# Mixes in four row strips, the first level ahead of the outputs, and a later logit stage

## The reference, cut to what matters

```python
xx = concatenate([zeros_like(x[:, :1]), x[:, :-1]], axis=1) - x
xxx = x + xx * maa_x
lora = tanh(xxx @ maa_w1).reshape(B, T, 5, 32)
m = einsum('btfd,fdc->fbtc', lora, maa_w2)      # mw, mk, mv, mr, mg
xw = x + xx * (maa_w + mw)                      # and xk, xv, xr, xg alike
r, k, v = xr @ Wr, xk @ Wk, xv @ Wv
g = tanh(xg @ gate_w1) @ gate_w2
w = time_decay + tanh(xw @ decay_w1) @ decay_w2
wdec = exp(-exp(w))
y = wkv6(r, k, v, wdec, u)                      # S = w*S + k v', y = r (S + u k v')
out = (norm(y) * g) @ Wo
```

## Time and profile before

| | us |
|---|---|
| median of three runs (lowest, highest) | 3041.12 (3040.53, 3043.16) |
| the profiled execution, whole time | 3043.45 |
| its span in the trace | 3041.6 |
| route a, up to the last scatter | 0 to 229 |
| experts a | 236 to 1164 |
| mix_and_route | 1171 to 2096 |
| experts b | 2101 to 3041 |

### The profile page before, as it was taken

How to read it: one execution, slowest core, us unless ns; L and a number is a source line. 1 busy time by engine, 2 the same in 40 slices (tenths; PEclk the granted TensorE clock), 3 DMA queues, 4 the chain that set the end, 5 groups by cost and what they waited for, 6 DMA issues and landing times. The chain is left out here.

```text
span 3041.6 us, 63629 instructions
## 1 busy us (share of the span) xinstructions
PE 2764.8 (91%) x21994; PEld 2212.3 (73%) x21994; DVE 1997.8 (66%) x4620; ACT 1575.5 (52%) x2733; POOL 1265.8 (42%) x1072
## 2 busy tenths in 40 slices
PE   6536999999999995899999999984999999999997
PEld 6535888888888883466666666663888888888886
DVE  5545666666666652688989898864666666566664
ACT  5424666666665652344444444432666656656663
POOL 2671322322222223457777777753222222232233
PEclk9999999999999997999999999997999999999998
DMA  9925545545544526201111111014455445445444
GB/s 343 334 94 116 91 81 89 94 77 88 95 78 86 96 33 222 98 16 44 35 53 33 54 33 55 26 38 116 82 89 95 77 86 95 79 86 94 80 70 149
DMA packets 540965, 281.28 MB, mean 92 GB/s; under 512 B 397591, under 2 KB 503131, under 8 KB 540480
## 3 DMA queue, kind: packets, MB, share of 16 engines
q1 hardware_dynamic: 478624, 202.67, 26.8%
q0 software_dynamic: 57888, 75.16, 14.6%
q10 hardware_dynamic: 4224, 0.52, 0.1%
HBM read 150.83 MB, written 146.41 MB: 98 GB/s over the span
## 5 line engine op out<-in xcount | busy, mean ns | idle before, releaser
L763 POOL DMA_INDIRECT acc_a<-ae_ob,ae_to x160 | 260.8, 1630 | 675.0 <-ACT ae_ob L712 623.0
L763 POOL DMA_INDIRECT acc_b<-be_ob,be_to x150 | 242.7, 1618 | 637.3 <-ACT be_ob L712 578.7
L730 ACT ACTIVATE be_h<-be_pH,b 128x512 f32<-128x512 f32 (+1 forms) x384 | 236.8, 617 | 359.2 <-PE be_pH L657 337.5
L730 ACT ACTIVATE ae_h<-ae_pH,b 128x512 f32<-128x512 f32 (+1 forms) x384 | 236.7, 616 | 342.1 <-PE ae_pH L657 324.1
L1478 POOL TENSOR_TENSOR m_xf<-m_tmp,m_xT 128x512 f32<-128x512 f32 x160 | 174.9, 1119 | 151.6 <-DVE m_tmp L1185 85.1
L1529 POOL DMA_INDIRECT slots_b<-m_row,m_sidx x128 | 143.1, 1118 | 109.3 <-issue 106.2
L1788 PEld LDWEIGHTS m_PP<-m_RP,m_KS 64*64 64x64 f32 x6656 | 115.6, 134 | 87.5 <-issue 86.4
L464 POOL DMA_INDIRECT slots_a<-ar_row,ar_sidx x128 | 126.0, 984 | 99.7 <-issue 73.8
L1788 PE MATMUL m_PP<-m_RP,m_KS 64*64 64x64 f32 x6656 | 130.0, 221 | 26.5 <-DVE m_A L1215 26.3
L657 PE MATMUL ae_pH<-ae_xT0h,ae_w_0h 128*128 128x512 f32 (+1 forms) x256 | 87.8, 343 | 69.3 <-DVE ae_xT0l L839 65.5
L1185 DVE SCALAR_TENSOR_TENSOR m_tmp<-m_B,m_ch,m_xx 128x512 f32<-128x512 f32 x160 | 114.0, 741 | 48.8 <-PE m_B L1895 38.5
(11 more groups left out here) (347 smaller groups left out, 9007.8 us busy)
## 6 DMA issues: line engine op xcount, KB each, us to landing
ae_stage<-in_w SPq DMA_DIRECT2D x64, 512.0 KB, 3.6
be_stage<-in_w SPq DMA_DIRECT2D x64, 512.0 KB, 3.5
slots_a<-empty SPq DMA_DIRECT2D x5, 4160.0 KB, 25.0
slots_b<-empty SPq DMA_DIRECT2D x5, 4160.0 KB, 31.6
ae_xq<-slots_a SPq DMA_DIRECT2D x252, 64.0 KB, 2.7
be_xq<-slots_b SPq DMA_DIRECT2D x252, 64.0 KB, 2.7
ar_xin<-in_x SPq DMA_DIRECT2D x16, 512.0 KB, 10.0
m_xin<-acc_a SPq DMA_DIRECT2D x16, 512.0 KB, 4.6
```

Source lines behind the costliest of these rows:

```text
L730: t = act.activation(dst[:, 0:SIZES[b]], pH[c % 2][:, 0:SIZES[b]], ACT.Gelu, bias=S.b1[:, bass.ds(i * (2 * FC) + (u * FC + f), 1)])
L763: pool.indirect_dma_start(S.acc[tag][:, :], bass.IndirectOffsetOnAxis(ap=to[m][:, q:q + 1], axis=0), ob[m][:, q, :], None, bounds_check=T ...
```

## The change

In `mix_and_route`:

- `mix_of` deals M0 to M3 as the first halves of features 0, 4, 1 and 2, one for each strip of 32 rows of TensorE, and M4 to M7 as the second halves. Four of them are issued in a row, into four banks.
- `narrow` writes both products into one bank, DW (partitions 0 to 63 and 64 to 127), and ACT takes the tanh of both in one instruction. It stands behind `updates(K)` now, and `rate(F, 0)` behind level 2.
- `level(F, 0)` is issued at the end of the step ahead of the outputs, where `level(L, 0)` stood at the head of the next one; on DVE its `take` stands behind the four `mix_in`s, ahead of both `add_out`s.
- `low_rest(X)` goes ahead of level 7 on PE, its tanh ahead of `assemble_left` on ACT; `places(R)` goes ahead of `gated(K)` on DVE.
- POOL computes `root_spread` (the power) ahead of `gate`. Nothing else of POOL's order is changed.

In `route`: the logits of a group and the copies ahead of them come a step later, and SP issues three of the 4160 KB DMAs after four loads, and the other two after two more.

```diff
--- before.py
+++ after.py
@@ -205,11 +205,15 @@
                         sp.wait_ge(xn_ready, g - XRING + 1)
                     sp.dma_start(xin[g % XRING][:, :, :], x_grp[g]).then_inc(x_loaded[g % XRING], 16)
 
-                for g in range(XRING):
+                for g in range(4):
                     load(g)
-                    if XRING - PAIRS <= g:
-                        S.empty_rows(sp, tag, g - (XRING - PAIRS))
-                for g in range(XRING, NG):
+                for j in range(3):
+                    S.empty_rows(sp, tag, j)
+                for g in range(4, 6):
+                    load(g)
+                for j in range(3, PAIRS):
+                    S.empty_rows(sp, tag, j)
+                for g in range(6, NG):
                     load(g)
                 for dst, src in S.mix.loads:
                     sp.dma_start(dst, src).then_inc(weights_loaded, 16)
@@ -415,8 +419,8 @@
                         turn(s + 3)
                     if 0 <= s + 1 < NG:
                         prefix(s + 1)
-                    if 0 <= s + 3 < NG:
-                        logits(s + 3)
+                    if 0 <= s + 2 < NG:
+                        logits(s + 2)
 
             @block.scalar
             def _(act):
@@ -441,7 +445,8 @@
                 for s in STEPS:
                     if 0 <= s + 3 < NG:
                         normalise(s + 3)
-                        copy_turned(s + 3)
+                    if 0 <= s + 2 < NG:
+                        copy_turned(s + 2)
                     if 0 <= s + 1 < NG:
                         g = s + 1
                         act.wait_ge(dif_ready, g + 1)
@@ -1045,13 +1050,12 @@
             for name, g in ((ROUTE, s - 2), (IN, s + 2)):
                 if live(g):
                     roots[name, g] = 3 * len(roots) + 3
-            order = [("M4", s + 1, a), ("M5", s + 1, b), ("DW", s + 1, c), ("GW", s + 1, d),
-                     ("U", s - 1, c), ("M6", s + 1, a), ("M7", s + 1, b),
-                     ("WA", s + 1, d), ("G0", s, a), ("K0", s + 1, b), ("K1", s + 1, a),
+            order = [("M4", s + 1, b), ("M5", s + 1, c), ("M6", s + 1, a), ("M7", s + 1, d),
+                     ("U", s - 1, b), ("DW", s + 1, c), ("WA", s + 1, d), ("G0", s, a), ("K0", s + 1, c), ("K1", s + 1, a),
                      ("WB", s + 1, d), ("G1", s, c), ("Y0", s - 1, b), ("Y1", s - 1, a),
                      ("M8", s + 1, d), ("M9", s + 1, c), ("L", s - 2, b), ("V0", s + 1, d), ("V1", s + 1, c),
                      ("LT", s - 2, b), ("R0", s + 1, a), ("R1", s + 1, d), ("LA", s + 2, c), ("C", s - 2, b), ("LG", s + 2, a),
-                     ("M0", s + 2, c), ("M1", s + 2, d), ("O0", s - 1, a), ("M2", s + 2, c), ("M3", s + 2, d),
+                     ("M0", s + 2, a), ("M1", s + 2, b), ("M2", s + 2, c), ("M3", s + 2, d), ("O0", s - 1, a),
                      ("O1", s - 1, b)]
             if not live(s):
                 order = [f for f in order if f[0] != "C"] + [f for f in order if f[0] == "C"]
@@ -1109,9 +1113,9 @@
 
         def mix_of(m):
 
-            return (STRIPS[m // 4 * 2 + m % 2], m // 2 % 2) if m < 8 else (REST, m - 8)
-
-        last_use = {0: "DW", 4: "GW", 1: "K1", 2: "V1", 3: "R1"}
+            return (STRIPS[m % 4], m // 4) if m < 8 else (REST, m - 8)
+
+        last_use = {0: "DW", 4: "DW", 1: "K1", 2: "V1", 3: "R1"}
         mixes = {f: 1 + max(m for m in range(10) if mix_of(m)[0] == f) for f in range(5)}
         heads = lambda t: t[:, :, :].rearrange("p q (h n) -> p (q h) n", n=N)
         flat = lambda t: t[:, :, :].rearrange("p c t -> p (c t)")
@@ -1392,7 +1396,6 @@
 
                 for s in STEPS:
                     L, F, X, K, R, Z = s, s + 1, s + 2, s - 1, s - 2, s - 3
-                    keep(L, 0)
                     if live(R):
                         norm_route(R)
                     if live(F):
@@ -1437,20 +1440,17 @@
                         choose(R)
                     factors(L, 5)
                     keep(L, 6)
+                    if live(R) and live(L):
+                        places(R)
                     if live(K) and live(L):
                         gated(K)
                     factors(L, 6)
-                    if live(R) and live(L):
-                        places(R)
                     if live(X):
-                        for m in range(2):
+                        for m in range(4):
                             mix_in(X, m)
+                    keep(F, 0)
                     if live(K):
                         add_out(K, 0)
-                    if live(X):
-                        for m in range(2, 4):
-                            mix_in(X, m)
-                    if live(K):
                         add_out(K, 1)
                     if live(R) and not live(L):
                         places(R)
@@ -1565,8 +1565,8 @@
                         for m in range(8, 10):
                             mix_add(F, m)
                     if live(K) and live(L):
+                        root_spread(K)
                         gate(K)
-                        root_spread(K)
                     if live(Z):
                         scatter(Z, (1,))
                     if live(L):
@@ -1647,9 +1647,8 @@
                 def narrow(g):
                     filled(act, "WB", g - 2)
                     filled(act, "G1", g - 2)
-                    for name, rows in (("DW", slice(0, N)), ("GW", slice(N, P))):
-                        filled(act, name, g)
-                        drains(act.activation(twg[g % 2][rows, :], bank(name, g)[rows, :], ACT.Tanh), name, g)
+                    filled(act, "DW", g)
+                    drains(act.activation(twg[g % 2][:, :], bank("DW", g)[:, :], ACT.Tanh), "DW", g)
 
                 def keys(g):
                     turned(act, KRT, g - 2)
@@ -1744,10 +1743,10 @@
                         shares(R)
                     if live(X):
                         low(X, "LA", lora[:, :])
+                    if live(X):
+                        low(X, "LG", lorag[:, :])
                     if live(L):
                         assemble_left(L)
-                    if live(X):
-                        low(X, "LG", lorag[:, :])
                     if live(K):
                         filled(act, "O1", K - 1)
                         filled(act, "L", R)
@@ -1913,12 +1912,12 @@
                 def narrow(g):
                     pe.wait_ge(mixed, g * 10 + mixes[0])
                     pe.wait_ge(mixed, g * 10 + mixes[4])
-                    b = {name: fill(name, g) for name in ("DW", "GW")}
+                    b = fill("DW", g)
                     for k in range(DC):
-                        for name, w, f, o in (("DW", dw1, 0, 0), ("GW", gw1, 4, N)):
-                            t = pe.matmul(b[name][o:o + N, :], w[:, k, :], xf[f][:, k, :], start=(k == 0), stop=(k == 1))
-                            if k == 1:
-                                fills_up(t, name, g)
+                        for w, f, o in ((dw1, 0, 0), (gw1, 4, N)):
+                            t = pe.matmul(b[o:o + N, :], w[:, k, :], xf[f][:, k, :], start=(k == 0), stop=(k == 1),
+                                          tile_position=(0, o), skip_group_check=True)
+                    fills_up(t, "DW", g)
 
                 def project(g, name, w, f):
                     pe.wait_ge(mixed, g * 10 + mixes[f])
@@ -1946,7 +1945,7 @@
                     fills_up(t, f"V{a}", g)
 
                 def gates(g, a):
-                    drained(pe, "GW", g)
+                    drained(pe, "DW", g)
                     b = fill(f"G{a}", g)
                     for q in range(2):
                         ts = slice((2 * a + q) * P, (2 * a + q + 1) * P)
@@ -1988,13 +1987,10 @@
 
                 for s in STEPS:
                     L, F, X, K, R = s, s + 1, s + 2, s - 1, s - 2
-                    if live(L) and L:
-                        level(L, 0)
                     if live(K):
                         turn_keys(K)
                     if live(F):
-                        mixes_of(F, range(4, 6))
-                        narrow(F)
+                        mixes_of(F, range(4, 8))
                     idle_last(L, 1)
                     if live(L):
                         level(L, 1)
@@ -2004,11 +2000,11 @@
                         updates(K)
                     idle_last(L, 3)
                     if live(F):
-                        mixes_of(F, range(6, 8))
-                    if live(F):
-                        rate(F, 0)
+                        narrow(F)
                     if live(L):
                         level(L, 2)
+                    if live(F):
+                        rate(F, 0)
                     if live(L):
                         gates(L, 0)
                     if live(R) and live(L):
@@ -2061,11 +2057,13 @@
                         low(X)
                     if live(R) and live(L):
                         prefix(R)
+                    if live(X):
+                        low_rest(X)
```

(15 more changed lines are left out.)

## The result

The changed kernel took 3113.61 us (median of four runs, 3107.10 to 3117.41), the kernel before 3041.61 us beside it (3040.53 to 3043.16). The ratio is 1.0235, with a 95% interval from 1.0217 to 1.0252. The forecast was 3112 us. Every ratio here compares the runs that lie up to 1.5% above the fastest run of their kernel.

What follows compares the result with a forecast made beforehand. The prediction took PE, DVE and POOL, going round together in a 51.24 us step of mix_and_route, as the bound. Its terms summed as 3041.1 + 74 (mix steps) - 3 (route a) = 3112 us, range 3050 to 3148.

Steps and rivals of the forecast that it cites:

- Part 1: mix_and_route, new deal of mixes: narrow starts 15.0 us after the first mix_add, PE waits about 6.8 us each full step.
- Part 2: PE behind narrow: the granted clock falls to 0.50 after the wait, losing 2.0 us in each step.
- Part 3: From narrow to DVE's factors 3: 20.75 us, including the 2.0 us lost to the clock.
- Part 4: Factors 3 to first mix_add: 21.15 us against 21.9, from -0.8 (mixes), -2.15 (factors 4), +2.2 (gate meeting choose).
- the rival in which the power holds DVE up: Factors 4 stands up to 3.4 us longer under the power, a step takes 2.9 more, 3144 us; chance 0.08.
- The sum: A step of mix_and_route takes 56.9 us against 51.24, +5.7; eleven make 63, with the other groups +74 us.
- Part 5: Route a: the fifth empty part lands earlier, -3 us, with bounds of +1 and -10.
- POOL is not late: Sixth mix_add ends within 8.2 us of the first, narrow does not wait; 3.2 us saved a step, 2991 us; chance 0.13.
- The wait is cheap: The wait comes, but the clock stays up and gate meets nothing: step 53.45 us, whole 3064 us; chance 0.14.
- no change: The wait is eaten by work DVE and POOL had to do anyway: 3035 to 3047 us; chance 0.05.

Runs made afterwards that it cites:

- the old deal: The changed kernel with mix_of dealing the mixes as before, run twice on the second chip: 1.0203 and 1.0184 of the kernel before.
- the kernel with both edits: The changed kernel with POOL's root_route and mix_adds 4 to 7 ahead of the totals, and mix_of dealing as before: 1.0029 of the kernel before.
- the turned order: POOL runs root_route, mix_adds 4 to 7, then the totals: 1.0227 put into the changed kernel, 1.0102 put into the kernel before.
- the kernel with both edits and gate first: The kernel with both edits, plus gate ahead of root_spread again, on the third chip: 1.0010 of the kernel before.
- the kernel whose waits were filled: The changed kernel with seven products without use issued on PE ahead of narrow's wait, second chip: 1.0260 of the kernel before.

## Why the prediction was right, point by point

**Part 1.** Right. The forecast was narrow 15.0 us after the first mix_add and a wait of 6.8; it came at 15.04 us, with waits of 6.1 us in the mean (61.1 us in ten, 1350 to 1900) and 6.40 in the step shown. PE was there 8.6 us after the first mix_add instead of 8.2. The "4 us of cover (level 1, updates)" was misread, those two take 1.9 us in the earlier trace rows; it enters no sum. The four products in four row strips took 1.14 us (forecast 1.2, bounds 1.05 and 2.1), for eight instructions, which two groups of four make. With the old deal on the second chip the same eight took 1.99.

**Part 2.** Right in kind, a little small in size: 2.4 us behind narrow instead of 2.0.

**Part 3.** Narrow to factors 3 was forecast at 20.75 us and took 1576.08 - 1555.89 = 20.19. One thing I missed works the other way from Part 2: rate 0 and gates 0 now stand one behind the other in PE's queue, with level 2 no longer between them. They have a contraction of 64 each, in different halves of TensorE's rows (partitions 0 to 63 and 64 to 127 of `twg`), and run at the same time. Both start at 1561.23, and the two together take 1.2 us, where the sum had 1.05 each, one behind the other.

**Part 4.** Factors 3 to the first mix_add was forecast at 21.15 and took 1597.12 - 1576.08 = 21.04 (the next first mix_add starts at 1597.12). Its terms are in DVE's and POOL's rows:

```profile
1576.08 0.70 DVE L1232 TENSOR_TENSOR m_RP<-m_RP,m_tot 128x512 f32<-128x512 f32 x1 [2.30 <-PE m_PP L1787]
...
1584.00 0.70 DVE L1243 TENSOR_TENSOR m_KS<-m_KS,m_tot 128x512 f32<-128x512 f32 x1
...
1586.85 2.38 DVE L1312 CAST m_ef<-m_topi 128x8 f32<-128x8 uint32 x1
```

```profile
1583.56 3.31 POOL L1501 TENSOR_TENSOR m_rvar<-m_mvar,m_minus_half 128x16 f32<-128x16 f32 x1
1586.86 2.34 POOL L1518 TENSOR_TENSOR m_Y<-m_Y,m_G 128x1024 f32<-128x1024 f32 x1
```

Factors 4 lies wholly inside the power and takes 0.70 us, so the rival in which the power holds DVE up is out, at 0.08 rightly low. The rule of the Trainium skill (SBUF — State Buffer, section "SBUF: two separate sides"), by which a GpSimd instruction blocks a VectorE instruction with two SBUF inputs for its whole length, agrees here with factors 4 under gate (2.83 us), and with factors 4 under the power (0.70 us) not at all. The cast of `choose` stands 2.38 us under gate, forecast 2.2.

**The sum.** A step was forecast at 56.9 us and took 56.26: +5.0 instead of +5.7. Eleven of them make 55 us instead of 63, and the groups at the ends cost 15 instead of 12. That 15 is itself a sum of misses: the first four steps cost 5.8 us instead of the 11.6 that I had for all groups outside the eleven, the stretch up to the first level 0 is 2.1 us shorter, and the one behind the last level 0 is 10.4 longer, which I had not counted. The stage's +69.8 stands against +74. I was 4 us too high there, and 2.8 us of gains in the two expert stages, whose code is not touched, were not in the sum. My difference of +71 us stands against +72.0 between the medians and +63.7 between the two profiled executions (3043.45 and 3107.10), which are what the terms can be compared with. So the median's agreement to 2 us is in part luck; the terms agree to 7.

**Part 5.** Right: -3.4 us, forecast -3, and by itself 0.9984.

**The rivals.** *POOL is not late* was tried by moving POOL's adds and the deal. The condition was right (the wait goes), the price was not: instead of 48.0 us the step came out at 50.5, with DVE busy 92.5% and PE 93.7%. My 2991 us had PE's savings count in full. *The wait is cheap* and *no change* are out by the trace.

What I did not see was the spread between chips: 3114 and 3214 us for one program, where the kernel before differed by 42 us. My range of 3050 to 3148 would not have held on the second chip. Of those 42 us the route has 45 (the last scatter of route a starts at 269.40 us in the kernel with both edits, at 224.68 in its like on the third chip), so the mix of the kernel before is most likely as fast there, but no trace of it was taken on that chip.

## What to carry to other kernels

When a product is moved behind a later result, count the distance from the first to the last operation that has to come before it on every engine, in the order of that engine's queue. Here 14.9 us on POOL decided against 8.6 on PE (8.2 forecast), and the profile before had both. A wait also costs the clock behind it, at 1.6 us now and then and at 2.8 us each time, in the traces here. Where such a wait is cured by turning the waited-for engine's queue, look at who read what was turned behind: the turned order took 1.9 hundredths of the kernel before's time off in one kernel and added 1.0 in the other.

## What the runs showed of the hardware

- The clock was at 0.50 behind waits of 6.4 us and of 2.8 us in every step looked at. Behind one of 1.62 (level 7 in the kernel before) it stayed at 1.00. Behind one of about 1.6 in the kernel with both edits and gate first it stayed at 1.00 in most steps and fell to 0.50 for 17 us in two, with PE at work all that time at half rate.
- Products in four row strips of 32 ran four at a time: eight instructions in 1.14 us, which four took in two strips before (1.13); eight in two strips took 1.99.
- On the second chip PE showed gaps of mostly 0.36 to 0.46 us inside runs of small products, always around a pair of POOL's scatters, but not around every pair, and none from 1440 to 1860 in the kernel with both edits. Where waits elsewhere had been, half the clock came behind some of them; in the kernel whose waits were filled it did not from 1500 on. That chip's route a is also 45 us longer: there POOL stands five times for some 8.9 us ahead of a scatter, again with no releaser, as in the row below, and no such row is in the trace of the third chip.

```profile
152.35 0.98 POOL L469 DMA_INDIRECT slots_a<-ar_row,ar_sidx  x1 [8.85 <-issue]
```

- An 8-column cast stood 2.38 us under a POOL product of two tensors, a 512-column product of DVE took 2.83 there instead of 0.69. Under a POOL power of 3.3 us the same cast took 0.17 and the same product 0.70.
